# A cross-interaction network on one core: W1 and W2 loaded with h on the partitions, in rows of 256 bytes, instead of being turned on TensorE

## The chip, the core and the metric

The kernel runs on one core of one Trainium2 chip. The metric is the device time of one execution in microseconds (us); three runs of the kernel before gave a median of 1092.18 us (1091.85 to 1092.72). One more execution was profiled; its trace is what the rows below come from.

## The reference, cut to what matters

```python
# input: (B=512, F=64, D=16);  W0: (128, 64*64), W1, W2: (128, 128*64);  b*: (128,)
x_vec = input
for W, b in ((W0, b0), (W1, b1), (W2, b2)):
    z = einsum('bhd,bfd->bhfd', x_vec, input).reshape(B, h * f, D)
    x_vec = einsum('oc,bcd->bod', W, z) + b[None, :, None]
    outs.append(x_vec.sum(axis=2))
y = concatenate(outs, axis=1)            # (512, 3 * 128)
```

In layers 1 and 2 the sum over c is a sum over h (128 outputs of the layer before) and f (64 fields). TensorE sums over the partitions, so a weight that it uses must stand with h on the partitions; in memory a row o of W1 or W2 holds h times f values, f innermost.

## The kernel before, in words

A tile is 8 samples of the batch times 16 elements, 128 columns; four tiles are a group, and there are 16 groups (0 "first", 1 to 14 "inner", 15 "last"). On every engine the code is a hand-written order: `body(n, kind)` runs over the 64 steps e = 0 to 63 of a group, with tile j and chunk c from `divmod(e, 16)`; tables of steps such as `LATER_AT` say at which e other work stands. Engines meet through semaphores.

Layer 0 makes products z of two fields (SyncE copies rows of xg into z, GpSimd multiplies, L453), which TensorE multiplies with W0 into the bank l0 (`layer0`, 17 tiles of z to a group, every second one split by ScalarE, L526, and VectorE, L718, into an upper and a lower part). The result is split into x1h and x1l.

Layer 1: W1 lies in SBUF as w1h and w1l (upper and lower part), 16 chunks of 4 fields times 128 outputs. A chunk of a tile is three matmuls of 512 columns (`chunk`, `by_parts`, L913) into one of four banks y; then each of its four fields is scaled with x0t and added up, for five chunks of 16 by ScalarE (`multiply`, L673) and GpSimd (L461 to L474), for the others by VectorE (`add_fields`, L769; for chunks 3 and 15 ScalarE scales in place, L662, and VectorE adds, L754).

Layer 2 needs only the sum over the elements. For each tile `layer2` (L1033) makes x2 times the inputs, which ScalarE puts into gram (L563). After each quarter of the batch `quarter` (L1021) multiplies gram with w2t, 64 matmuls of 128 columns in fp32, each of two passes in the trace, with `w2t[:, f, :]` stationary: eight parts of eight fields between the chunks of steps 18 to 25 of groups 4, 8 and 12, and the last quarter at the very end. ScalarE's L571 then reads the sum.

The start: SyncE loads W1 in eight parts of 512 KB, in rows of 4 KB, into w1raw, which is the space of w2t, with o on the partitions (L387). Each chunk is turned by four transposes on TensorE (`turn_w1`, L968) into l2p, from which ScalarE makes w1h (`w1_upper`, L588) and VectorE w1l (`w1_lower`, L777). Two chunks are turned ahead (`W1_AHEAD`); each of steps 0 to 13 of group 0 turns one more ahead of its chunk, and chunk c of tile 0 waits for w1l of c. ScalarE loads W2 into w2raw, the space of gram, at steps 0, 1, 3, 4, 6, 7, 9 and 10 of group 0 (`load_w2`, L595). At steps 14 to 29 of group 0 TensorE turns W2 (`turn_w2`, L1010) and ScalarE copies it into w2t (`w2_out`, L582). Tile 0 of group 0 is done with the group's first 128 columns, whose layer 0 was made early; the other 384 (LATER) have their layer 0 at steps 3 to 13 of tile 0, with SyncE's copies held until the first six parts of W1 have landed, and tile 1 waits for their x1h and x1l (L735, step 14 on VectorE).

Of the kernel before, what the change touches and what calls it, by code (L numbers as in the profile page):

```python
# [12 lines left out]
B, F, D = 512, 64, 16  # L13
# [64 lines left out]
W2_AT = 14  # L78
# [6 lines left out]
W2_LOAD_AT = [k * 3 // 2 for k in range(W_PARTS)]  # L85
# [23 lines left out]
def layer2_at(n, j):  # L109

    return LAYER2_AT + 2 if n == 0 and j == 1 else LAYER2_AT


# [5 lines left out]
def cin_kernel(nc, x, w0, b0, w1, b1, w2, b2, out):  # L119
    with ExitStack() as ctx:  # L120
# [12 lines left out]
        w2t = sb("w2t", [P, F, O])  # L133
# [32 lines left out]
        w1raw = w2t[:].rearrange("p f o -> p (f o)")  # L166
        w2raw = gram[:].rearrange("p f b -> p (f b)")
# [4 lines left out]
        w0raw = w2raw[:, 0:F * F]  # L172
# [3 lines left out]
        w0pair, w0pair_left = w2raw[:, F * O - (ZT - 1) * P:], scratch[:, 4 * F:4 * F + ZCOPIES * ZLAST]  # L176
# [25 lines left out]
        w1_turned = sem("w1_turned")  # L202
# [10 lines left out]
        w2_turned = sem("w2_turned")  # L213
        w2_kept = sem("w2_kept")
# [144 lines left out]
        def _(sp):  # L359
# [68 lines left out]
        def _(pool):  # L428
# [13 lines left out]
            nc.gpsimd.memset(w2raw[:, F * F:(F + F // 2) * F], 0.0).then_inc(w0_spare_set, 1)  # L442
# [61 lines left out]
        def _(act):  # L504
# [74 lines left out]
            def w2_out(c):  # L579

                act.wait_ge(w2_turned, c + 1)
                nc.scalar.copy(w2t[:, CF * c:CF * c + CF, :], l2p[:, c % 2, :].rearrange("p (f o) -> p f o", o=O)) \  # L582
                    .then_inc(w2_kept, 1)
# [12 lines left out]

            def body(n, kind):
                act.wait_ge(x0t_made, 2 * n + 1)
                for e in range(TILES * CHUNKS):
# [4 lines left out]
                    if kind == "first" and e in W2_LOAD_AT:  # L604
                        load_w2(W2_LOAD_AT.index(e))
# [101 lines left out]
        def _(dve):  # L707
# [146 lines left out]
            for r in range(W0_STEPS - 1):  # L854
                if r == W0_STEPS - 2:
# [9 lines left out]
                          at(w2raw, F * F - F * s0, [-F, n], [F + 1, half - 1]))  # L865
# [38 lines left out]
        def _(pe):  # L904
# [53 lines left out]
            def turn_w1(k):  # L958

                if k == 0:  # L960
                    pe.wait_ge(w1_loaded, 16 * W1_FIRST)
                    pe.wait_ge(w1_rest_loaded, 16 * (W_PARTS - W1_FIRST))
                    pe.wait_ge(early_left_lowered, 1)
                    pe.wait_ge(early_z_made, W0_STEPS - 1)
                if k >= 2:
                    pe.wait_ge(w1l_made, k - 1)
                for i in range(CF):
                    last = nc.tensor.transpose(l2p[:, k % 2, i * O:(i + 1) * O],  # L968
                                               w1raw.rearrange("o (h f) -> o f h", f=F)[:, CF * k + i, :], ident[:])
                last.then_inc(w1_turned, 1)  # L970

# [32 lines left out]
            def turn_w2(c):  # L1004
                if c >= 2:
                    pe.wait_ge(w2_kept, c - 1)
                else:
                    pe.wait_ge(w1l_made, CHUNKS)
                for k in range(CF):
                    last = nc.tensor.transpose(l2p[:, c % 2, k * O:(k + 1) * O],  # L1010
                                               w2raw.rearrange("o (h f) -> o f h", f=F)[:, CF * c + k, :], ident[:])
                last.then_inc(w2_turned, 1)
# [55 lines left out]
            for k in range(W1_AHEAD):  # L1068
                turn_w1(k)
            pe.wait_ge(wh_made, W0_STEPS)  # L1070

            def body(n, kind):
                for e in range(TILES * CHUNKS):
# [9 lines left out]
                    if kind == "first" and e + W1_AHEAD < CHUNKS:  # L1083
                        turn_w1(e + W1_AHEAD)
# [5 lines left out]
                    if kind == "first" and W2_AT <= e < W2_AT + CHUNKS:  # L1090
                        if e == W2_AT:
                            pe.wait_ge(w2_loaded, 16 * W_PARTS)
                        turn_w2(e - W2_AT)
                    if c == layer2_at(n, j) and (kind != "first" or j > 0):
                        if kind == "first" and j == 1:
                            pe.wait_ge(w2_kept, CHUNKS)
                        layer2(tile - 1, (j - 1) % 2)
# [49 lines left out]
```

## Time and profile before

| what | value |
|---|---|
| median of three runs | 1092.18 us (1091.85 to 1092.72) |
| the profiled execution | 1091.6 us |
| span of its trace | 1089.5 us |
| TensorE busy (matmul) | 1064.6 us, 98% of the span |
| VectorE, GpSimd, ScalarE busy | 877.3, 859.6, 710.3 us |
| mean share of the DMA engines in group 0's first tile (26 to 60 us) | 0.87 |

About 2 us of the profiled execution lie outside the span. PE stands for TensorE's matmuls and PEld for its loads of stationary operands, which overlap with them; DVE is VectorE, ACT ScalarE, POOL GpSimd, SP SyncE, and a q behind an engine's name its issuing of DMAs. Times in a trace count from the span's start. Before some 120 us the engines wait for each other and for transfers; after that TensorE has hardly a gap until the last quarter.

### The profile page before, as it was taken

The page shows a single profiled execution, that of the slowest core. Times are in us where ns is not written, and L with a number is a line of the kernel's source. Part 1 is how long each engine was busy: PE and PEld are TensorE (multiplying, and loading weights), DVE is VectorE, ACT ScalarE, POOL GpSimd, SP SyncE. Part 2 cuts the span into 40 slices and gives each one's busy share as a digit, 9 for nine tenths or more (in the row PEclk, how much of TensorE's full clock was granted, in tenths as well). Part 3 has the DMA queues.
Part 4 walks back from the last instruction along what each step waited for, and adds up shares of the span by engine and source line. Part 5 has one row for each costly group of instructions (what it writes and reads, how often), then busy time and mean ns, then how long its engine had stood idle before and what let it go on. Part 6 is the DMA issues. An engine that isn't in the chain of part 4 may idle for free.

```text
span 1089.5 us, 18056 instructions
## 1 busy us (share of the span) xinstructions
PE 1064.6 (98%) x4783; PEld 803.5 (74%) x4783; DVE 877.3 (81%) x2673; ACT 710.3 (65%) x2447; POOL 859.6 (79%) x727
## 2 busy tenths in 40 slices
PE   5999999999999999999999999999999999999997
PEld 5777777777778777777778777777778877777676
DVE  5768989889874888989894798989886598888881
ACT  4666767676764767767673676777675576767770
POOL 2668997989884897989985799898987589898550
PEclk9999999999999999999999999999999999999998
DMA  7942423332322323323241232433332133320000
GB/s 275 245 92 81 101 71 71 96 76 78 66 70 58 76 78 69 85 57 97 66 87 40 56 97 66 88 84 69 94 79 59 47 69 97 76 79 28 1 23 8
DMA packets 108327, 85.88 MB, mean 79 GB/s; under 512 B 71040, under 2 KB 73824, under 8 KB 108096
## 3 DMA queue, kind: packets, MB, share of 16 engines
q1 hardware_dynamic: 106832, 78.17, 29.3%
q10 hardware_dynamic: 1392, 6.55, 1.9%
q8 instruction: 38, 0.62, 0.2%
q14 instruction: 65, 0.53, 0.2%
HBM read 14.75 MB, written 0.79 MB: 14 GB/s over the span
## 4 chain that ended last, share of the span: by engine, by line
PE 90%; DVE 3%; ACT 2%; DMA 2%; POOL 1%; issue 1%; ACTq 0%; SPq 0%; DVEq 0%; POOLq 0%
PE y L913 62%; PE l L934 9%; PE l L913 8%; PE xt L1021 5%; PE l2p L1033 4%; DVE acc L769 2%; DMA gram<-in_L_rec_W_dram 1%; PE l2p L1010 1%; ACT y L662 1%; DMA z<-xg 1%; ACT prod L673 1%; POOL z L453 1%; DVE gram L851 1%; PE l L922 0%; POOL pacc L463 0%
## 5 line engine op out<-in xcount | busy, mean ns | idle before, releaser
L769 DVE SCALAR_TENSOR_TENSOR acc<-y,x0t,acc 128x128 f32<-128x128 f32 x2048 | 559.8, 341 | 101.8 <-PE y L913 99.1
L673 ACT ACTIVATE prod<-y,x0t 128x128 f32<-128x128 f32 x1280 | 365.8, 379 | 157.4 <-PE y L913 148.6
L913 PE MATMUL y<-w1h,x1h 128*128 128x512 f32 x1024 | 464.6, 454 | 2.2 <-DVE acc L769 1.4
L913 PE MATMUL y<-w1h,x1l 128*128 128x512 f32 x1024 | 402.1, 393 | 0.0
L913 PE MATMUL y<-w1l,x1h 128*128 128x512 f32 x1024 | 400.6, 391 | 0.0
L453 POOL TENSOR_TENSOR z<-z,xg 128x512 f32<-128x512 f32 (+2 forms) x272 | 352.5, 1300 | 32.8 <-DMA z<-xg 32.8
L463 POOL TENSOR_TENSOR pacc<-pacc,prod 128x512 f32<-128x512 f32 x192 | 268.0, 1396 | 79.7 <-ACT prod L673 78.3
L913 PEld LDWEIGHTS y<-w1h,x1h 128*128 128x128 f32 x1024 | 193.2, 189 | 96.8 <-issue 26.5
L662 ACT ACTIVATE y<-y,x0t 128x128 f32<-128x128 f32 x512 | 142.6, 342 | 157.4 <-PE y L913 157.2
L913 PEld LDWEIGHTS y<-w1l,x1h 128*128 128x128 f32 x1024 | 192.8, 188 | 59.3 <-issue 28.8
L913 PEld LDWEIGHTS y<-w1h,x1l 128*128 128x128 f32 x1024 | 192.1, 188 | 43.0
L754 DVE TENSOR_TENSOR acc<-y,acc 128x512 f32<-128x512 f32 x128 | 88.3, 690 | 64.6 <-ACT y L662 61.4
L718 DVE TENSOR_TENSOR zl<-z,zh 128x512 fp32r<-128x512 f32 (+1 forms) x128 | 126.9, 991 | 7.1 <-ACT zh L526 4.5
L934 PE MATMUL l<-z,w0t 128*128 128x512 f32 (+1 forms) x256 | 128.8, 584 | 0.0
L469 POOL TENSOR_TENSOR pacc<-pacc,acc 128x512 f32<-128x512 f32 x63 | 87.4, 1387 | 42.4 <-DVE acc L754 34.5
L461 POOL TENSOR_TENSOR pacc<-prod 128x512 f32<-128x512 f32 x64 | 90.0, 1406 | 37.7 <-ACT prod L673 37.5
L526 ACT CAST zh<-z 128x512 fp32r<-128x512 f32 (+1 forms) x128 | 81.4, 636 | 10.9 <-POOL z L453 7.7
L652 ACT ACTIVATE bd<-x0t,own_half 128x64 f32<-128x64 f32 x256 | 69.1, 359 | 0.0
L1021 PEld LDWEIGHTS xt<-gram,w2t 128*128 128x128 f32 x512 | 62.3, 195 | 3.6 <-ACT sums L565 1.5
L1021 PE MATMUL xt<-gram,w2t 128*128 128x128 f32 x512 | 62.7, 279 | 0.8 <-ACT sums L565 0.8
L767 DVE TENSOR_SCALAR acc<-y,x0t 128x128 f32<-128x128 f32 x192 | 54.9, 341 | 0.0
L934 PEld LDWEIGHTS l<-z,w0t 128*128 128x128 f32 x256 | 47.8, 188 | 9.6
(85 smaller groups left out, 673.0 us busy)
## 6 DMA issues: line engine op xcount, KB each, us to landing
z<-xg SPq DMA_DIRECT2D x480, 128.0 KB, 2.4
w2t<-in_L_rec_W_dram SPq DMA_DIRECT2D x8, 512.0 KB, 7.1
gram<-in_L_rec_W_dram ACTq DMA_DIRECT2D x8, 512.0 KB, 7.4
xg<-in_r_input_dram SPq DMA_DIRECT2D x30, 128.0 KB, 3.8
z<-xg SPq DMA_DIRECT2D x32, 96.0 KB, 5.9
z<-xg SPq DMA_DIRECT2D x15, 192.0 KB
gram<-in_L_rec_W_dram ACTq DMA_DIRECT2D x1, 2048.0 KB, 9.2
out_dram<-z SPq DMA_DIRECT2D x4, 192.0 KB, 1.9
```

The lines of the kernel that those rows point to most:

```text
L453: nc.gpsimd.tensor_tensor(to[0:rows, :], to[0:rows, :], xg[0:rows, cols], ALU.mult).then_inc(z_made, 1)
L461: nc.gpsimd.tensor_tensor(pacc[:], prod[:, 0], prod[:, 1], ALU.add).then_inc(pool_step, 1)
L463: nc.gpsimd.tensor_tensor(pacc[:], pacc[:], prod[:, h % HSLOTS], ALU.add).then_inc(pool_step, 1)
L469: nc.gpsimd.tensor_tensor(pacc[:], pacc[:], acc[:, slot], ALU.add).then_inc(pool_step, 1)
L662: last = nc.scalar.activation(of, of, ACT.Copy, scale=x0t[:, j, f:f + 1])
L673: last = nc.scalar.activation(prod[:, h % HSLOTS, k, :], y[c % YB][:, k * O:(k + 1) * O], ACT.Copy, scale=x0t[:, j, f:f + 1])
L718: nc.vector.tensor_tensor(zl[:, i % ZLSLOTS, cols], zin(n, t), zh[:, zhslot(n, t), cols].bitcast(F32), ALU.subtract).then_inc(zl_made, 1)
L754: nc.vector.tensor_tensor(to, y[c % YB][:], to, ALU.add).then_inc(acc_step, 1)
L769: ins = nc.vector.scalar_tensor_tensor(out=to, in0=of, scalar=x0t[:, j, f:f + 1], in1=b1r[:] if m == 0 else to, op0=ALU.mult, op1=ALU.add)
L913: ins = nc.tensor.matmul(to, stationary, moving, start=(first and k == 0), stop=(last and k == 2))
L934: nc.tensor.matmul(l0[:, cols], w0t[:, WHOLE.index(t), :], zin(n, t), start=(t == 0), stop=False).then_inc(z_used, 1)
L1021: last = nc.tensor.matmul(l2, w2t[:, f, :], gram[:, f, :], start=(f == 0), stop=(f == F - 1))
```

## The change

W1 and W2 are loaded by their DMAs straight into the layout with h on the partitions: `w2t` is now [h, o, f], part k of a load is 16 outputs o, and each piece that the DMA moves is one (o, h) row of 64 fields, 256 bytes (before, 4 KB). So the transposes `turn_w1` and `turn_w2` are gone, and `w2_out` with them. `w1_upper` and `w1_lower` take their chunk from SBUF, from w2t with a step of 64 elements from one o to the next, and write the same w1h and w1l. ScalarE's first one waits for all eight parts of W1. W2 goes into w2t itself, after W1 has been used up, in group 1 (steps 4, 11, ..., 53), and `quarter` reads `w2t[:, :, f]`, a step of 64 elements from column to column. `quarter(1)` waits for the load.

```diff
-W2_AT = 14
-W2_LOAD_AT = [k * 3 // 2 for k in range(W_PARTS)]
+W2_LOAD_AT = [4 + 7 * k for k in range(W_PARTS)]
-        w2t = sb("w2t", [P, F, O])
+        w2t = sb("w2t", [P, O, F])
-        w1raw = w2t[:].rearrange("p f o -> p (f o)")
+        w1raw = w2t[:].rearrange("p o f -> p f o")
...
-                    part = slice(k * F * O // W_PARTS, (k + 1) * F * O // W_PARTS)
-                    sp.dma_start(w1raw[:, part], w1[:, part]).then_inc(w1_loaded if k < W1_FIRST else w1_rest_loaded, 16)
+                    part = slice(k * O // W_PARTS, (k + 1) * O // W_PARTS)
+                    sp.dma_start(w2t[:, part, :], w1[part, :].rearrange("o (h f) -> h o f", f=F)) \
+                        .then_inc(w1_loaded if k < W1_FIRST else w1_rest_loaded, 16)
...
             def w1_upper(k):
-                act.wait_ge(w1_turned, k + 1)
-                nc.scalar.copy(w1h[:, k, :], l2p[:, k % 2, :]).then_inc(w1h_made, 1)
+                if k == 0:
+                    act.wait_ge(w1_loaded, 16 * W1_FIRST)
+                    act.wait_ge(w1_rest_loaded, 16 * (W_PARTS - W1_FIRST))
+                nc.scalar.copy(w1h[:, k, :].rearrange("p (f o) -> p f o", o=O),
+                               w1raw[:, CF * k:CF * k + CF, :]).then_inc(w1h_made, 1)
             def load_w2(k):
                 if k == 0:
-                    act.wait_ge(w0l_made, W0_STEPS - 1)
-                act.dma_start(w2raw[:, part], w2[:, part]).then_inc(w2_loaded, 16)
+                    act.wait_ge(w1l_made, CHUNKS)
+                act.dma_start(w2t[:, part, :], w2[part, :].rearrange("o (h f) -> h o f", f=F)).then_inc(w2_loaded, 16)
...
-                    if kind == "first" and e in W2_LOAD_AT:
+                    if n == 1 and e in W2_LOAD_AT:
                         load_w2(W2_LOAD_AT.index(e))
...
             def w1_lower(k):
-                nc.vector.tensor_tensor(w1l[:, k, :], l2p[:, k % 2, :], w1h[:, k, :].bitcast(F32),
-                                        ALU.subtract).then_inc(w1l_made, 1)
+                split = w1h[:, k, :].bitcast(F32).rearrange("p (f o) -> p f o", o=O)
+                nc.vector.tensor_tensor(w1l[:, k, :].rearrange("p (f o) -> p f o", o=O),
+                                        w1raw[:, CF * k:CF * k + CF, :], split, ALU.subtract).then_inc(w1l_made, 1)
...
             def quarter(q, part, fields_kept):
                 if part == 0:
+                    if q == 1:
+                        pe.wait_ge(w2_loaded, 16 * W_PARTS)
...
-                    last = nc.tensor.matmul(l2, w2t[:, f, :], gram[:, f, :], start=(f == 0), stop=(f == F - 1))
+                    last = nc.tensor.matmul(l2, w2t[:, :, f], gram[:, f, :], start=(f == 0), stop=(f == F - 1))
```

(`turn_w1`, `turn_w2`, `w2_out`, `layer2_at` and the semaphores between them are taken out; w2raw, which also holds W0, is named w0stage.)

On TensorE, where group 0 begins, there stood (L968 turns W1, L913 is a chunk):

```order
L985 MATMUL l0<-zh,w0left 128x128
L968 MATMUL l2p<-ident,w2t 128x128 x12
L913 MATMUL y0<-w1h,x1h 128x512
L913 MATMUL y0<-w1l,x1h 128x512
L913 MATMUL y0<-w1h,x1l 128x512
L968 MATMUL l2p<-ident,w2t 128x128 x4
L913 MATMUL y1<-w1h,x1h 128x512
```

and now stands (L901 is the chunk):

```order
L959 MATMUL l0<-zh,w0left 128x128
L901 MATMUL y0<-w1h,x1h 128x512
L901 MATMUL y0<-w1l,x1h 128x512
L901 MATMUL y0<-w1h,x1l 128x512
L901 MATMUL y1<-w1h,x1h 128x512
```

The twelve transposes ahead of the first chunk and the four ahead of each later one are gone; nothing takes their place on TensorE.

On VectorE, at the same place, there stood (L777 makes w1l, L769 and L767 add up chunk 1, L718 splits z):

```order
L735 SCALAR_TENSOR_TENSOR x1l<-l0,b0c,x1h 128x128
L777 TENSOR_TENSOR w1l<-l2p,w1h 128x512 x4
L769 SCALAR_TENSOR_TENSOR acc<-y1,x0t,b1r 128x128
L767 TENSOR_SCALAR acc<-y1,x0t 128x128 x3
L718 TENSOR_TENSOR zl<-z,zh 128x384
```

and now stands:

```order
L722 SCALAR_TENSOR_TENSOR x1l<-l0,b0c,x1h 128x128
L765 TENSOR_TENSOR w1l<-w2t,w1h 128x512 x4
L756 SCALAR_TENSOR_TENSOR acc<-y1,x0t,b1r 128x128
L754 TENSOR_SCALAR acc<-y1,x0t 128x128 x3
L705 TENSOR_TENSOR zl<-z,zh 128x384
```

The order is as before; the first operand of the sixteen instructions that make w1l is w2t in SBUF where it was l2p in PSUM.

On ScalarE, in group 1, the first of the eight loads of W2 now stands between work of step 3 and step 4 (L649 and L660 scale chunks); the rows that load W2 in group 0 are gone:

```order
L550 ACTIVATE x1h<-l0,b0c 128x128
L649 ACTIVATE y3<-y3,x0t 128x128 x4
L584 DMA w2t<-in_L0_rec_W2_dram 128x16x64
L660 ACTIVATE prod<-y0,x0t 128x128 x4
```

So the eight loads of W2 have moved from group 0 to group 1, into the order of the steps 4, 11, ..., 53.

## Rows read from the trace of the kernel before

**Rows 1.** The page: engines' busy time, and the chain that ended last

```profile
PE 1064.6 (98%) x4783; PEld 803.5 (74%) x4783; DVE 877.3 (81%) x2673; ACT 710.3 (65%) x2447; POOL 859.6 (79%) x727
PE 90%; DVE 3%; ACT 2%; DMA 2%; POOL 1%; issue 1%; ACTq 0%; SPq 0%; DVEq 0%; POOLq 0%
```

**Rows 2.** Windows: length, busy us (instructions), granted clock, DMA share, GB/s

```profile
26.00:60.00 34.00, 31.17 (x153) 24.98 (x153) 25.44 (x63) 20.91 (x57) 20.99 (x19) 1.00 0.87 214
60.00:119.00 59.00, 57.69 (x257) 43.33 (x257) 43.05 (x121) 40.77 (x125) 47.23 (x39) 1.00 0.39 93
```

**Rows 3.** Timeline of PE (start, us, instruction): transposes, and starts of tiles 0, 1 and 4

```profile
23.26 1.42 PE L968 MATMUL l2p<-ident,w2t 128*128 128x128 f32 x8 [0.89 <-issue]
26.17 0.48 PE L913 MATMUL y<-w1h,x1h 128*128 128x512 f32 x1
...
59.78 0.47 PE L913 MATMUL y<-w1h,x1h 128*128 128x512 f32 x1 [0.46 <-issue]
...
119.21 0.39 PE L913 MATMUL y<-w1h,x1h 128*128 128x512 f32 x1
```

**Rows 4.** The chain that ended last, in order of time: start, us, what

```profile
24.75 0.70 DVE w1l L777
...
33.58 7.98 DMA z<-xg
...
63.99 0.55 PE l2p L1010 x4
...
88.41 0.68 PE l L913 x3
...
90.44 0.86 PE l L934 x2
...
100.62 0.64 PE l2p L1033 x4
```

**Rows 5.** Groups by shape on DVE, 0 to 120 us: count, busy us, mean ns, idle before

```profile
L777 DVE TENSOR_TENSOR w1l<-l2p,w1h 128x512 fp32r<-128x512 f32 x16 | 10.9, 683 | 3.8 <-ACT w1h L588 3.8
L718 DVE TENSOR_TENSOR zl<-z,zh 128x512 fp32r<-128x512 f32 x8 | 9.9, 1238 | 0.6 <-ACT zh L526 0.5
L851 DVE TENSOR_TENSOR gram<-gram 128x256 f32<-128x256 f32 x8 | 5.0, 629 | 0.3
L888 DVE TENSOR_TENSOR w0l<-gram,w0h 128x256 fp32r<-128x256 f32 x4 | 1.5, 422 | 0.1
```

**Rows 6.** Timeline of PEld: eight loads from contiguous columns, eight with 256 bytes between

```profile
15.84 0.97 PEld L977 LDWEIGHTS l<-prod,gram 128*128 128x128 f32 x8
...
23.23 1.25 PEld L968 LDWEIGHTS l2p<-ident,w2t 128*128 128x128 f32 x8 [1.00 <-issue]
```

**Rows 7.** Groups on PE and PEld, 0 to 120 us, columns as in rows 5

```profile
L968 PE MATMUL l2p<-ident,w2t 128*128 128x128 f32 x64 | 11.8, 310 | 1.8 <-DVE w1l L777 0.9 <-issue 0.9
L968 PEld LDWEIGHTS l2p<-ident,w2t 128*128 128x128 f32 x64 | 11.1, 245 | 3.7 <-issue 2.1 <-DVE w1l L777 0.4
L977 PEld LDWEIGHTS l<-prod,gram 128*128 128x128 f32 x24 | 2.9, 191 | 0.0
```

**Rows 8.** The chain: one part of a quarter and the chunk behind it

```profile
319.52 1.78 PE xt L1021 x16
321.31 0.70 PE y L913 x3
```

**Rows 9.** The page's DMA issues: KB each, median us to landing

```profile
z<-xg SPq DMA_DIRECT2D x480, 128.0 KB, 2.4
w2t<-in_L_rec_W_dram SPq DMA_DIRECT2D x8, 512.0 KB, 7.1
xg<-in_r_input_dram SPq DMA_DIRECT2D x30, 128.0 KB, 3.8
```

**Rows 10.** Line 402, SyncE's loads of xg: issue time ns min/median/max

```profile
L402 SPq DMA_DIRECT2D xg<-in_r_input_dram x30: 650/912/1532, 53.0 to 938.7; - x30
```

**Rows 11.** Groups on ACT, as in rows 5

```profile
L588 ACT CAST w1h<-l2p 128x512 fp32r<-128x512 f32 x16 | 9.4, 592 | 3.5 <-PE l2p L968 3.4
```

More of the change, by code:

```diff
@@ L106, in zslot @@
     return t % ZSLOTS
-def layer2_at(n, j):
-    return LAYER2_AT + 2 if n == 0 and j == 1 else LAYER2_AT
 def last_in(t, slots):
@@ L163, in cin_kernel @@
         sums2_from_1 = sums[:].rearrange("p l b -> p (l b)")[:, 2 * B - QB:]
-        w1raw = w2t[:].rearrange("p f o -> p (f o)")
-        w2raw = gram[:].rearrange("p f b -> p (f b)")
+        w1raw = w2t[:].rearrange("p o f -> p f o")
+        w0stage = gram[:].rearrange("p f b -> p (f b)")
         zfirst = [prod[:, i] for i in range(HSLOTS)] + [acc[:, 0]]
@@ L171, in cin_kernel @@
         xraw = zflat[0:GROUP_B, 0:2 * F * D]
-        w0raw = w2raw[:, 0:F * F]
+        w0raw = w0stage[:, 0:F * F]
         zturned = zflat[:, ZSLOTS * GROUP - (ZT - 1) * P:]
@@ L175, in cin_kernel @@
         xturned, zturned_left = scratch[:, 0:2 * F], scratch[:, 2 * F:2 * F + ZCOPIES * ZLAST]
-        w0pair, w0pair_left = w2raw[:, F * O - (ZT - 1) * P:], scratch[:, 4 * F:4 * F + ZCOPIES * ZLAST]
+        w0pair, w0pair_left = w0stage[:, F * O - (ZT - 1) * P:], scratch[:, 4 * F:4 * F + ZCOPIES * ZLAST]
         outs = zflat[:, 0:(B // P) * L * O].rearrange(
@@ L201, in cin_kernel @@
         pair_step = sem("pair_step")
-        w1_turned = sem("w1_turned")
         w1_rest_loaded = sem("w1_rest_loaded")
@@ L212, in cin_kernel @@
         w0left_made = sem("w0left_made")
-        w2_turned = sem("w2_turned")
-        w2_kept = sem("w2_kept")
         xg_loaded = sem("xg_loaded")
@@ L441, in _ @@
                                     pattern=[[D, TILE_B]], channel_multiplier=-1).then_inc(consts_made, 1)
-            nc.gpsimd.memset(w2raw[:, F * F:(F + F // 2) * F], 0.0).then_inc(w0_spare_set, 1)
+            nc.gpsimd.memset(w0stage[:, F * F:(F + F // 2) * F], 0.0).then_inc(w0_spare_set, 1)
             def product(n, t):
@@ L577, in row_out @@
                 nc.scalar.copy(outs[:, r, :], l0[:, 0:L * O]).then_inc(outs_made, 1)
[L579 to L583, printed above, removed]
             def w1_upper(k):
-                act.wait_ge(w1_turned, k + 1)
-                nc.scalar.copy(w1h[:, k, :], l2p[:, k % 2, :]).then_inc(w1h_made, 1)
+                if k == 0:
[3 more added lines that the diff above has]
+                               w1raw[:, CF * k:CF * k + CF, :]).then_inc(w1h_made, 1)
             def load_w2(k):
                 if k == 0:
-                    act.wait_ge(w0l_made, W0_STEPS - 1)
-                part = slice(k * F * O // W_PARTS, (k + 1) * F * O // W_PARTS)
-                act.dma_start(w2raw[:, part], w2[:, part]).then_inc(w2_loaded, 16)
+                    act.wait_ge(w1l_made, CHUNKS)
+                part = slice(k * O // W_PARTS, (k + 1) * O // W_PARTS)
+                act.dma_start(w2t[:, part, :], w2[part, :].rearrange("o (h f) -> h o f", f=F)).then_inc(w2_loaded, 16)
             def body(n, kind):
@@ L617, in body @@
                         scale(tile, j, c)
-                    if kind == "first" and W2_AT <= e - 1 < W2_AT + CHUNKS:
-                        w2_out(e - 1 - W2_AT)
-                    if c == layer2_at(n, j) + 1 and (kind != "first" or j > 0):
+                    if c == LAYER2_AT + 1 and (kind != "first" or j > 0):
                         before = (n * TILES + (j - 1) + QG * TILES) % (QG * TILES) if kind != "first" else j - 1
@@ L864, in _ @@
                           at(w0raw, F - s0, [-1, n], [F + 1, half - 1]),
-                          at(w2raw, F * F - F * s0, [-F, n], [F + 1, half - 1]))
+                          at(w0stage, F * F - F * s0, [-F, n], [F + 1, half - 1]))
                 add_pairs(at(w0pair, F * s0, [F, n], [1, half]),
@@ L956, in turn_w0 @@
                 last.then_inc(prep_made, 1)
[L958 to L970, printed above, removed]
             def early_layer0(r):
@@ L1002, in turn_row @@
                 last.then_inc(turned, 1)
[L1004 to L1012, printed above, removed]
             def quarter(q, part, fields_kept):
@@ L1067, in _ @@
             early_left()
-            for k in range(W1_AHEAD):
-                turn_w1(k)
             pe.wait_ge(wh_made, W0_STEPS)
@@ L1082, in body @@
                         pe.wait_ge(l2_used, (n // QG if kind == "inner" else 0) + 1)
-                    if kind == "first" and e + W1_AHEAD < CHUNKS:
-                        turn_w1(e + W1_AHEAD)
                     if kind == "first" and j == 0:
@@ L1089, in body @@
                         turn_row(ROWS_AT.index(e))
[L1090 to L1096, printed above, removed]
+                    if c == LAYER2_AT and (kind != "first" or j > 0):
                         layer2(tile - 1, (j - 1) % 2)
```

## The prediction

> **What bounds the kernel now.** I read the page first: TensorE is busy for 98% of the span, and the chain that ended last is TensorE for 90% [rows 1]. From that alone, taking transposes off TensorE saves their time. But an average hides stages, so I read windows and starts of tiles next. Tile 0 of group 0 runs from 26.17 to 59.78, 33.6 us, tiles 1 to 3 from 59.78 to 119.21, 59.4 us [rows 3], while a tile without z work beside it holds 16 chunks of about 0.70 us, some 11 us [rows 8]. In 26 to 60 TensorE shows 31.2 us busy, yet VectorE has 25.4 and the DMA engines 0.87 [rows 2], and the chain goes there through a transfer of z (7.98 us at 33.58), not through TensorE alone [rows 4]. So I count three stages apart: tile 0, where several engines are near their limit; tiles 1 to 3, where TensorE is; and the other fifteen groups, where TensorE alone counts and each nanosecond added to it is added to the end. I then looked for rows that show what a step of 256 bytes costs a reader of SBUF, since the change brings three such readers.
>
> **W1's arrival.** Before, TensorE starts to turn W1 at 23.26 [rows 3], so W1 has landed by then. The same 4 MB now come as 16,384 pieces of 256 bytes instead of 1,024 of 4 KB. The nearest rows: 128 KB in 64 pieces of 2 KB (z from xg) land after 2.4 us, 128 KB in 2,048 pieces of 64 bytes (xg) after 3.8 [rows 9], so 2,000 more pieces take 1.4 us more. Each of the eight parts has 2,048 pieces. Lower bound: the pieces hide behind the bytes, nothing. Upper bound: 8 x 1.4 = 11 us. I take 4 us, nearer to the lower end since bytes and pieces are moved by the same engines together: W1 is there at 27. The issues, 0.65 to 1.5 us for as many pieces [rows 10], total at most 12 us from 8.6 on and are done before.
>
> The Trainium skill, page "DMA: Bandwidth & Descriptors", section "Specifications", asks for at least 512 bytes in a transfer for the full rate and says that smaller ones are read, modified and written. By that W1 would come at some half of its rate, near the upper bound; no row here has pieces of 256 bytes.
>
> **Tile 0.** TensorE loses 16 blocks of four transposes, 0.55 us each [rows 4], and ScalarE and VectorE no longer wait for them. But w1l changes its price. Before, it reads one operand from PSUM and takes 683 ns [rows 5]. Now both are in SBUF, one with 256 bytes between its elements. A subtraction with both in SBUF, contiguous, of 256 elements takes 422 ns (L888); an addition of 256 with steps of 260 bytes takes 629 (L851) [rows 5]. The step costs 207 ns per 256 elements, so 414 per 512: 683 + 414 = 1.10 us. Bounds: 0.68, if one strided operand is free, and 2 x 629 = 1.26. Besides, an operation with both operands in SBUF and GpSimd at work beside it averages 1,238 ns for 512 elements (L718) [rows 5], 0.55 above 683; GpSimd is busy for 21 of 34 us here [rows 2], so I add half, 0.25. That makes 1.35 us, with 0.68 and 1.8 as ends. ScalarE's copies, 592 ns from PSUM [rows 11], have no row for a strided read from SBUF: between 0.6 and, with VectorE's increase, 1.0 us; ScalarE has 13 us to spare in this stage [rows 2], so only the first is on the path.
>
> VectorE's work: of 25.44 us in 26 to 60, fourteen w1l are 9.6, so 15.9 are other work [rows 2, 5]. Sixteen at 1.35 are 21.6; the sum is 37.5 us. It starts at 27 + 1.0 = 28.0 instead of 24.75 [rows 4]; with 2 us of waits (z copies begin later, but no longer share the DMA engines with W2) tile 1 starts at 67.5 instead of 59.78: **7.7 us later**. TensorE's freed 9 us buy nothing here; VectorE is late next.
>
> **Tiles 1 to 3.** Fourteen blocks of four transposes go, and the waits for ScalarE's copies between them. What is left for TensorE: 48 chunks at 0.70, 33.6; eight tiles of z at 0.86 and eight at 0.68 for group 1, 12.3; three `layer2` at 0.64 and what follows them, about 0.85 each, 2.5; turning fields and the last tile of z 0.6 [rows 4, 8]: 49.0. GpSimd needs 47.2 of its own [rows 2], so it nearly binds; I take 50.5 instead of 59.4: **8.9 us saved**. Group 1 then starts at 118.0 instead of 119.2.
>
> **W2 in group 1.** Eight issues on ScalarE, 0.65 to 1.5 us each going by the loads of xg [rows 10], in front of ScalarE's multiplies, for which the banks y wait. Hidden while ScalarE (65% busy [rows 1]) is ahead; TensorE has four banks, 2.8 us, to run on. Bounds 0 and 8 x 0.65 = 5; I take **1 us**. `quarter(1)` is three groups later, so its wait costs nothing.
>
> **The quarters.** Each of 512 passes of L1021 loads 128 columns of w2t, now with 256 bytes from column to column. A part of sixteen takes 1.78 us on the chain, 0.111 each [rows 8], and that is also the pitch of loads from contiguous columns, (0.97 - 0.19) / 7 [rows 6, 7]: the loads, not the matmuls, set it. L968 loads W1 with the very step that w2t has now, 64 elements: (1.25 - 0.25) / 7 = 0.143 [rows 6, 7], and the eight matmuls on them take (1.42 - 0.31) / 7 = 0.159 with the first gap in it [rows 3, 7], 0.31 being the mean length of one. I take 0.146. So 512 x 0.0345 = **17.7 us more**, in stages where TensorE has no idle time to absorb it; VectorE and GpSimd only idle longer. Bounds: 0, if the load hides behind a matmul of two passes; by the blocks of 0.55 for four (0.138) 13.6; if each load's extra length (245 against 191 ns, rows 7) shows in full, 27.6.
>
> The Trainium skill, page "TensorE: Matmul & The Clock Gate", section "LDWEIGHTS (loading the stationary operand)", gives a load's time from its number of columns alone; by that the step would be free and this term nothing. Rows 7 disagree, 245 against 191 ns for as many columns.
>
> **The sum.** +7.7 - 8.9 + 1 + 17.7 = +17.5 us on a span of 1089.5 and a profiled execution of 1091.6; the median of the runs is 0.6 above that. 1092.2 + 17.5 = 1109.7; I say 1109.
>
> **Rivals.**
> 1. *VectorE and GpSimd take the stride for nothing* (w1l at 0.95 us, with the contention alone). For it: no row has one strided operand beside a contiguous one; in L851 both are strided and in the same tile. Tile 0 then needs 15.2 + 15.9 = 31 us on VectorE and tile 1 starts near 61: 1102 to 1103.
> 2. *Pieces of 256 bytes are paid one by one.* W1 is there at 34, 7 us later, and z's copies, held until six parts are there, as well: 1116, up to 1120 if VectorE also waits for GpSimd in full (1.8 us). For it: 64-byte pieces cost 1.4 us a part; against it: those rows include no queue of parts.
> 3. *The strided loads hide in the quarters*, the other side: the pitch stays 0.111, the 17.7 us fall away, and the time is 1092, no change; with rival 1 as well, 1085, faster. It decides from the point where a pass's matmul takes longer than 0.146. For it: in L968's blocks the matmul is one pass of another kind; against it: the pitch of L1021 equals that of bare contiguous loads. The skill's rule on columns would have this result.
> 4. That the change does not do what it says is no rival: both transposes are gone from TensorE's order, and what reads w2t is there with its step. Only the gain in tile 0 is in doubt, above.
>
> **How the numbers follow.** The forecast 0.53 (its own range 1103 to 1114), rival 1 0.18, rival 2 0.17, rival 3 0.12, of which 0.05 faster, 0.04 within 0.2% and 0.03 slower (a part of the 17.7 left). From the forecast's bounds and rivals 1 and 2, the range is 1098 to 1121; it leaves out rival 3 and the end of rival 2. About 0.2% is what a measurement of this kernel can tell from no change; that is 2.2 us. Faster 0.05, within it 0.05, slower 0.90.
>
> **What would show it.** In the changed kernel's profile: the parts of a quarter near 2.3 us on the chain, the last quarter longer by some 4 us; w1l near 1.1 us where GpSimd is idle and more beside it; tile 1 starting near 67, with VectorE busy throughout tile 0; group 1 starting near 118; W1 landed near 27. Wrong would be: quarters unchanged in pitch, then rival 3; w1l under 0.8, then rival 1; the first chunk after 35, then rival 2; TensorE idle in group 1 at the issues of W2 by more than 5 us.

## The result, and the profile after

| | before | after |
|---|---|---|
| median of four runs, side by side | 1092.45 us (1091.85 to 1093.49) | 1148.47 us (1148.06 to 1148.94) |
| span of the profiled execution | 1089.5 us | 1146.0 us |

The changed kernel is 5.1% slower: the ratio is 1.0512, 95% interval 1.0494 to 1.0530. The sign was right; the size was not: 1109 was forecast with a range to 1121, and the loss is 56 us instead of 17.

I read the trace of the changed kernel in the order of the prediction, by stages. In the new lines, a chunk is L901, `w1_upper` L576, `w1_lower` L765, a quarter L987, the load of W1 L378. First the timeline of TensorE (start, us, instruction): the first matmul of tile 0, of tile 1, of group 1 and of group 2; it answers to [rows 3].

```profile
34.07 0.76 PE L901 MATMUL y<-w1h,x1h 128*128 128x512 f32 x1 [9.42 <-DVE w1l L765]
...
74.75 0.47 PE L901 MATMUL y<-w1h,x1h 128*128 128x512 f32 x1 [0.59 <-issue]
...
124.39 0.39 PE L901 MATMUL y<-w1h,x1h 128*128 128x512 f32 x1
...
186.47 0.39 PE L901 MATMUL y<-w1h,x1h 128*128 128x512 f32 x1
```

Against [rows 3], tile 0 starts 7.9 us later and takes 40.7 us instead of 33.6; tiles 1 to 3 take 49.6 instead of 59.4; group 1 takes 62.1 where its counterpart, from 119.21 to 181.04, took 61.8. So at group 2 the changed kernel is 5.4 us behind, of 56. The rest lies in the four quarters. The chain that ended last (start, us, what) shows it, beside [rows 8]:

```profile
324.95 3.40 PE xt L987 x16
328.35 0.70 PE y L901 x3
329.05 3.40 PE xt L987 x16
```

A part of sixteen passes takes 3.40 us instead of 1.78, 0.2125 us a pass instead of 0.111, and a chunk beside it is unchanged. Each of the groups 4, 8 and 12 is 12.9 us longer (87.8 against 74.8), and the last quarter, which has nothing beside it, 12.2. The groups on the two pages (count, busy us, mean ns, idle before) say the same of the loads, first in the changed kernel, then in the kernel before:

```profile
L987 PEld LDWEIGHTS xt<-gram,w2t 128*128 128x128 f32 x512 | 114.6, 311 | 2.5 <-ACT sums L557 1.5
```

```profile
L1021 PEld LDWEIGHTS xt<-gram,w2t 128*128 128x128 f32 x512 | 62.3, 195 | 3.6 <-ACT sums L565 1.5
```

The start, on the chain, and then in windows (length; busy us and instructions of PE, PEld, DVE, ACT and POOL; granted clock, DMA share, GB/s), as in [rows 2]:

```profile
21.02 2.52 SPq L378
...
23.58 7.73 DMA w2t<-in_L_rec_W_dram
...
31.38 1.07 ACT w1h L576
...
32.47 1.35 DVE w1l L765
```

```profile
20.00:24.00 4.00, 3.23 (x29) 3.02 (x28) 2.94 (x10) 2.55 (x9) 0.00 (x0) 1.00 1.35 219
26.00:34.00 8.00, 0.00 (x0) 0.00 (x0) 1.53 (x2) 2.62 (x3) 2.01 (x2) 0.55 1.02 198
34.00:75.00 41.00, 33.75 (x90) 20.52 (x91) 40.20 (x63) 26.39 (x56) 28.35 (x21) 0.75 0.35 79
75.00:124.00 49.00, 48.93 (x200) 34.86 (x200) 40.88 (x120) 32.65 (x111) 46.96 (x38) 1.00 0.43 104
```

The last piece of W1 lands at 31.3, its eighth issue having begun only at 23.6: each issue holds SyncE for some 2.3 us. While W1 comes in pieces of 256 bytes the DMA engines are busy without a pause and move 219 GB/s (20 to 24 us). In the kernel before, with rows of 4 KB, they moved 419:

```profile
16.00:20.00 4.00, 3.57 (x32) 3.38 (x32) 3.76 (x10) 2.63 (x10) 0.00 (x0) 1.00 1.03 419
```

At 219 GB/s a part of 512 KB takes 2.4 us, about as long as an issue is held, so issues and transfers go at one pace. An issue of as many pieces took 0.37 us in group 1, where the loads stood some 7 us apart, so it is not slow in itself; that it waits for the transfers ahead of it is the likelier reading, and is not shown.

While TensorE waits, its granted clock falls to 0.55, a mix of its two levels (1.2 and 2.4 GHz), and it is 0.75 in tile 0. But in tile 0 VectorE is busy for 40.20 of 41 us: it sets the end there. In tiles 1 to 3 TensorE is busy throughout, as forecast.

The groups of VectorE and ScalarE up to 120 us, beside [rows 5, 11], and after them the lower part of z of the same shape in the kernel before:

```profile
L765 DVE TENSOR_TENSOR w1l<-w2t,w1h 128x512 fp32r<-128x512 f32 x16 | 23.8, 1500 | 7.7 <-ACT w1h L576 7.7
L705 DVE TENSOR_TENSOR zl<-z,zh 128x384 fp32r<-128x384 f32 x8 | 8.1, 1008 | 0.0
L576 ACT CAST w1h<-w2t 128x512 fp32r<-128x512 f32 x16 | 17.3, 1100 | 6.3 <-DMA w2t<-in_L_rec_W_dram 6.3
```

```profile
L718 DVE TENSOR_TENSOR zl<-z,zh 128x384 fp32r<-128x384 f32 x8 | 5.6, 696 | 6.2 <-ACT zh L526 3.9 <-PE l L934 2.3
```

### The profile page after: what moved, and what is told of

The parts are those of the page before. It is cut to its first block, busy times and chain, and to the rows that moved or that the text cites. A ratio compares the mean times of both kernels' runs of the same rounds, so it can differ in the third digit from the quotient of the medians.

```text
span 1146.0 us, 17779 instructions
## 1 busy us (share of the span) xinstructions
PE 1109.0 (97%) x4655; PEld 842.2 (73%) x4655; DVE 890.5 (78%) x2673; ACT 708.9 (62%) x2431; POOL 867.1 (76%) x727
## 4 chain that ended last, share of the span: by engine, by line
PE 86%; DVE 4%; issue 3%; POOL 2%; SPq 1%; ACT 1%; DMA 1%; ACTq 0%; DVEq 0%; POOLq 0%
PE y L901 57%; PE xt L987 10%; PE l L922 8%; PE l L901 7%; PE l2p L999 3%; DVE acc L756 2%; SPq L378 1%; DVE w1l L765 1%; POOL z L445 1%; POOL pacc L455 1%; DMA w2t<-in_L_rec_W_dram 1%; ACT y L649 1%; POOL pacc L453 1%; DVE zl L705 1%; DVE acc L741 0%
## 5 line engine op out<-in xcount | busy, mean ns | idle before, releaser
L901 PE MATMUL y<-w1h,x1h 128*128 128x512 f32 x1024 | 466.9, 456 | 14.5 <-DVE w1l L765 11.6
L660 ACT ACTIVATE prod<-y,x0t 128x128 f32<-128x128 f32 x1280 | 365.7, 380 | 182.8 <-PE y L901 172.8
L901 PE MATMUL y<-w1h,x1l 128*128 128x512 f32 x1024 | 403.8, 394 | 0.0
L901 PE MATMUL y<-w1l,x1h 128*128 128x512 f32 x1024 | 403.0, 394 | 0.0
L445 POOL TENSOR_TENSOR z<-z,xg 128x512 f32<-128x512 f32 (+2 forms) x272 | 359.4, 1326 | 33.3 <-DMA z<-xg 33.3
L901 PEld LDWEIGHTS y<-w1h,x1h 128*128 128x128 f32 x1024 | 193.5, 189 | 117.3 <-issue 38.0
L649 ACT ACTIVATE y<-y,x0t 128x128 f32<-128x128 f32 x512 | 142.6, 342 | 158.5 <-PE y L901 158.5
L901 PEld LDWEIGHTS y<-w1l,x1h 128*128 128x128 f32 x1024 | 194.0, 189 | 59.7 <-issue 28.8
L901 PEld LDWEIGHTS y<-w1h,x1l 128*128 128x128 f32 x1024 | 193.4, 189 | 43.2
L461 POOL TENSOR_TENSOR pacc<-pacc,acc 128x512 f32<-128x512 f32 x63 | 87.8, 1393 | 40.5 <-DVE acc L741 32.6
L987 PEld LDWEIGHTS xt<-gram,w2t 128*128 128x128 f32 x512 | 114.6, 311 | 2.5 <-ACT sums L557 1.5
L987 PE MATMUL xt<-gram,w2t 128*128 128x128 f32 x512 | 113.8, 379 | 0.7 <-ACT sums L557 0.7
```

The lines of the kernel that those rows point to most:

```text
L445: nc.gpsimd.tensor_tensor(to[0:rows, :], to[0:rows, :], xg[0:rows, cols], ALU.mult).then_inc(z_made, 1)
L461: nc.gpsimd.tensor_tensor(pacc[:], pacc[:], acc[:, slot], ALU.add).then_inc(pool_step, 1)
L649: last = nc.scalar.activation(of, of, ACT.Copy, scale=x0t[:, j, f:f + 1])
L660: last = nc.scalar.activation(prod[:, h % HSLOTS, k, :], y[c % YB][:, k * O:(k + 1) * O], ACT.Copy, scale=x0t[:, j, f:f + 1])
L901: ins = nc.tensor.matmul(to, stationary, moving, start=(first and k == 0), stop=(last and k == 2))
L987: last = nc.tensor.matmul(l2, w2t[:, :, f], gram[:, f, :], start=(f == 0), stop=(f == F - 1))
```

## Experiments

### One part alone: only the quarters' layout

The kernel before, with both transposes left in place; only w2t has o ahead of f, so that a quarter reads every 64th element.

```diff
-        w2t = sb("w2t", [P, F, O])
+        w2t = sb("w2t", [P, O, F])
...
-                    last = nc.tensor.matmul(l2, w2t[:, f, :], gram[:, f, :], start=(f == 0), stop=(f == F - 1))
+                    last = nc.tensor.matmul(l2, w2t[:, :, f], gram[:, f, :], start=(f == 0), stop=(f == F - 1))
```

> The kernel before, with one part of the change alone: w2t lies as [h, o, f] (ScalarE's copies of the turned W2 write with a step of 256 bytes) and the quarters read their stationary operand with that step; W1 and W2 are loaded and turned as before. Theory A, the step alone doubles the pitch of the quarters' 512 passes: 1092.4 + 512 x (0.2125 - 0.111) = 1144 us, with the parts of sixteen at 3.40 us on the chain. Rival B, the pitch comes from how the change fills w2t or from its transfers running beside it: the parts stay between 1.8 and 2.4 us and the time between 1092 and 1111.

Measured: 1146.28 us, ratio 1.0493 (1.0477 to 1.0508). Its chain in the first quarter:

```profile
323.65 3.40 PE xt L1022 x16
```

The layout alone gives 53.7 of the 56 us, at the same 3.40 us a part. By the spans it is 54.9 us, and 50.8 of them lie behind the start of group 2, which comes 4.1 us later than in the kernel before (185.14 against 181.04). Of these 4.1, 2.8 are tile 1, which went from 26.7 to 29.5 us, as ScalarE's copies into that layout went from 0.6 to 1.1 us and stand on its chain. Another 2.3 are a later first chunk (28.51 against 26.17 us) although nothing was changed ahead of it, so single traces of the start differ by some 2 us; tile 0 is 1.0 shorter.

### The other part alone: the quarters read a row again

The changed kernel, where a quarter's stationary operand is 128 elements in a row.

```diff
-                    last = nc.tensor.matmul(l2, w2t[:, :, f], gram[:, f, :], start=(f == 0), stop=(f == F - 1))
+                    last = nc.tensor.matmul(l2, w2t[:].rearrange("p o f -> p (o f)")[:, f * O:(f + 1) * O], gram[:, f, :], start=(f == 0), stop=(f == F - 1))
```

> The changed kernel with the quarters' stationary operand read from 128 contiguous columns of w2t; these are other values than layer 2 needs, so the layer's sums are not the reference's, the work is the same. Theory A, the step of the quarters is 51 of the 56 us: 1148.5 - 51 = 1097 us, 4 to 6 above the kernel before, and the parts of sixteen at 1.78 us. Rival B, as above: parts above 2.4 us and a time near 1148.

Measured: 1098.21 us, ratio 1.0053 (1.0038 to 1.0067); a part takes 1.78 us again.

```profile
325.10 1.78 PE xt L987 x16
```

So all the rest of the change costs 5 to 6 us, and 50 us hang on the step at which the quarters read w2t. Tile 0 still takes 40.5 us here (34.22 to 74.70); the next runs start from this kernel.

### How the price depends on the step

The changed kernel, with three of the quarters read at another step in each of their eight parts: 1, 2, 4, 8, 16, 32, 63 and 64 elements. The first quarter has the strided operand stationary, the second transposes it, the third has it moving.

```diff
+STEPS = (1, 2, 4, 8, 16, 32, 63, 64)
...
+                    step = STEPS[part]
+                    of = flat[:, f % step:f % step + step * (O - 1) + 1:step]
+                    if q == 1:
+                        last = nc.tensor.matmul(l2, of, gram[:, f, :], start=(f == 0), stop=(f == F - 1))
+                    elif q == 2:
+                        for _ in range(2):
+                            last = nc.tensor.transpose(l2, of, ident[:])
+                    else:
+                        last = nc.tensor.matmul(l2, gram[:, f, :], of, start=(f == 0), stop=(f == F - 1))
```

> The changed kernel, with its eight parts of a quarter reading w2t at steps of 1, 2, 4, 8, 16, 32, 63 and 64 elements in turn: in the first quarter as the stationary operand of the fp32 matmul, in the second as that of a transpose (two to a field, so sixteen to a part as well), in the third as the moving operand of the fp32 matmul, with gram stationary. The sums of these quarters are not the reference's. Theory A (a load is slowed by each new 16-byte line of SBUF, as the Trainium skill, page SBUF - State Buffer, section Specifications, has it): first quarter 1.8 us a part at steps 1 and 2 and 3.4 from step 4 on, 63 like 64. Rival B (banks: a step that is a power of two is what hurts): 63 near 1.8, and a growth over 8, 16, 32, 64. Second quarter: 2.35 us (0.147 each) at step 64 if a transpose loads faster than a pass of an fp32 matmul, as before; 3.4 if it was its surroundings that made it so. Third quarter: 1.8 us at each step if the moving operand has time to spare in a two-pass matmul; 3.4 at the long steps if it reads through the same limit.

The parts on the chain, for steps 1, 2, 4 and 64 with the operand stationary (L995), 32 and 64 as a transpose (L998), 1, 2 and 4 as the moving operand (L1000):

```profile
325.31 1.78 PE xt L995 x16
...
327.79 1.88 PE xt L995 x16
...
330.36 3.61 PE xt L995 x16
...
353.07 3.40 PE xt L995 x16
...
605.77 1.79 PE xt L998 x16
...
611.61 2.32 PE xt L998 x16
...
849.70 1.78 PE xt L1000 x16
...
852.18 1.82 PE xt L1000 x16
...
854.70 3.63 PE xt L1000 x16
```

For the fp32 matmul the price is a jump, not a slope. Up to a step of 2 elements (8 bytes) it is nothing or 0.1 us a part, from 4 elements (16 bytes) on the part takes 3.4 to 3.7 us at every step, and it makes no difference which of the two operands is strided. Sixteen transposes at the same steps take 1.75 to 1.96 us, and 2.32 only at 64. So a transpose is no proxy for a pass of an fp32 matmul: my row for the price was of the wrong kind of instruction.

The Trainium skill, page "SBUF — State Buffer", section "Specifications (TRN2)", has lines of 16 bytes and wants two hits in each for the full bandwidth; the jump between 8 and 16 bytes agrees with that. By its words alone the transposes should pay too, and from 4 to 32 elements they do not.

### Which read sets the pitch

The same three quarters, now with 128, 112, 96, 80, 64, 48, 32 and 16 moving columns: first W2 stationary at every 64th element (L996), then stationary in a row (L992), then gram stationary and W2 moving at every 64th element (L994).

```diff
+COLUMNS = (128, 112, 96, 80, 64, 48, 32, 16)
...
+                    if q == 2:
+                        last = nc.tensor.matmul(l2[:, 0:n], flat[:, f * O:(f + 1) * O], gram[:, f, 0:n], **ends)
+                    elif q == 3:
+                        last = nc.tensor.matmul(l2[:, 0:n], gram[:, f, :], w2t[:, 0:n, f], **ends)
+                    else:
+                        last = nc.tensor.matmul(l2[:, 0:n], w2t[:, :, f], gram[:, f, 0:n], **ends)
```

> The changed kernel with three forms of the quarter, part by part with 128, 112, 96, 80, 64, 48, 32 and 16 moving columns: the first quarter with W2 as the stationary operand at every 64th element, the second with W2 as the stationary operand in a row, the third with gram as the stationary operand and W2 moving at every 64th element; the last quarter is unchanged. The columns left out are not computed. If the read of the strided operand sets the pitch (twice 128 columns at 0.83 ns, 212 ns), the first quarter's parts of 16 stay at 3.4 us whatever the count of moving columns, and the third's fall with the count from 3.5 us to that of the stationary read, about 1.8 us, at 64. If the matmul itself is slower whatever is read, the first quarter's parts fall with the columns too. The second quarter's parts stay near 1.8 us if its stationary read sets the pitch, and fall below if the moving columns do.

From the chain, the parts with 128 and 16 columns of the first form, 16 of the second, and 128, 112, 80 and 64 of the third:

```profile
325.20 3.40 PE xt L996 x16
...
357.24 3.26 PE xt L996 x16
...
617.33 1.69 PE xt L992 x16
...
854.78 3.51 PE xt L994 x16
...
858.99 3.08 PE xt L994 x16
...
866.98 2.23 PE xt L994 x16
...
869.91 1.77 PE xt L994 x16
```

With the strided operand stationary the pitch does not follow the moving columns: the load sets it, 212 ns for 128 columns, 1.66 ns each, against 111 ns or 0.87 each in a row. With it moving, 16 columns fewer take 0.43 us off a part, 27 ns off a pass, 1.7 ns a column, until the contiguous load is the longer at 64 columns. Both readers pay about double for each column at this step. No order of the operands avoids it; another place in memory does.

### W1's small pieces

The kernel with contiguous quarter reads, and W1 loaded in rows of 4 KB as before.

```diff
-                    part = slice(k * O // W_PARTS, (k + 1) * O // W_PARTS)
-                    sp.dma_start(w2t[:, part, :], w1[part, :].rearrange("o (h f) -> h o f", f=F)) \
+                    part = slice(k * F * O // W_PARTS, (k + 1) * F * O // W_PARTS)
+                    sp.dma_start(w2t[:].rearrange("p o f -> p (o f)")[:, part], w1[:, part]) \
```

> As the kernel with contiguous quarters, and W1 loaded in rows of 4 KB as before the change, into the same space (so w1h and w1l hold values of W1 in wrong places); everything that reads w2t keeps its step. Theory A, the 256-byte rows delay W1 from 23 to 31 us and tile 0 with it: the first chunk starts 7 to 8 us earlier, near 26.5, tile 1 near 67 instead of 74.8, and the time is 1097 - 6 to 8 = 1090. Rival B, tile 0 is bound by VectorE and GpSimd whenever W1 comes: tile 1 starts less than 3 us earlier, and the time is 1095 or more.

Measured: 1090.94 us, ratio to the kernel before 0.9982 (0.9972 to 0.9992), 7.3 less than with the small pieces. On TensorE's timeline the first chunk starts 6.9 us earlier than at 34.22. The eight issues of the load (issue ns min/median/max, first and last start us), here and then in the changed kernel:

```profile
27.33 0.67 PE L901 MATMUL y<-w1h,x1h 128*128 128x512 f32 x1 [2.73 <-DVE w1l L765]
```

```profile
L378 SPq DMA_DIRECT2D w2t<-in_L_rec_W_dram x8: 328/572/1509, 8.1 to 13.7; - x8
```

```profile
L378 SPq DMA_DIRECT2D w2t<-in_L_rec_W_dram x8: 379/2324/3812, 8.1 to 23.6; - x8
```

The pieces of 256 bytes are nearly all of the late start, 6.9 of 7.9 us, and they show as issues that hold the queue. Tile 0 takes 39.5 us here (27.33 to 66.82) although the granted clock is 0.91 in it, not 0.75: the lower clock accounts for at most 1 of its 7 us.

### What makes tile 0 long: the step

The kernel with contiguous quarter reads, small pieces again; ScalarE and VectorE read 512 elements of w2t in a row.

```diff
-                               w1raw[:, CF * k:CF * k + CF, :]).then_inc(w1h_made, 1)
+                               w2t[:].rearrange("p o f -> p (o f)")[:, k * CHUNK:(k + 1) * CHUNK].rearrange("p (f o) -> p f o", o=O)).then_inc(w1h_made, 1)
...
-                                        w1raw[:, CF * k:CF * k + CF, :], split, ALU.subtract).then_inc(w1l_made, 1)
+                                        w2t[:].rearrange("p o f -> p (o f)")[:, k * CHUNK:(k + 1) * CHUNK].rearrange("p (f o) -> p f o", o=O), split, ALU.subtract).then_inc(w1l_made, 1)
```

> The kernel of the run with contiguous quarter reads (1098.2 us, tile 0 from 34.1 to 74.6), and in it ScalarE's and VectorE's 16 reads each of W1 are of 512 elements in a row instead of every 64th; so w1h and w1l hold other values of W1 than they should, and the numbers computed are not the reference's. If the stride is what made tile 0 longer (40.5 us against 33.6 before), ScalarE's copy falls from 1.10 to about 0.6 us and VectorE's difference from a mean of 1.5 to 0.7 to 0.9 us, tile 0 takes 33 to 35 us and the time is about 1092. If tile 0 is long because the layer 0 operations around it and GpSimd set its pace, the instructions get shorter, tile 0 stays at 38 us or more and the time at 1096 or more.

Measured: 1093.23 us, ratio 1.0009 (0.9999 to 1.0018); tile 0 takes 36.7 us (32.96 to 69.66). Neither expectation held in full. ScalarE's copy takes 0.62 us, but the differences fell less than expected; one line of them (ns min/median/max, first and last start):

```profile
L765 DVE TENSOR_TENSOR w1l<-w2t,w1h x16: 677/1482/1760, 32.0 to 66.3; 128x512 fp32r<-128x512 f32 x16
```

Two prices stand in that row, so I set VectorE's timeline in the changed kernel (start, us) beside GpSimd's:

```profile
44.25 1.06 DVE L765 TENSOR_TENSOR w1l<-w2t,w1h 128x512 fp32r<-128x512 f32 x1
...
45.82 1.82 DVE L765 TENSOR_TENSOR w1l<-w2t,w1h 128x512 fp32r<-128x512 f32 x1
```

```profile
45.55 1.28 POOL L453 TENSOR_TENSOR pacc<-prod 128x512 f32<-128x512 f32 x1 [3.56 <-ACT prod L660]
46.80 1.67 POOL L445 TENSOR_TENSOR z<-z,xg 128x384 f32<-128x384 f32 x1
```

With GpSimd idle the strided difference takes 1.06 us; with GpSimd at work through it, 1.82. In the contiguous run the two are 0.68 and mostly 1.49 (of the twelve with GpSimd beside them one takes 1.05, and two, which began just ahead of a GpSimd instruction or in its last 0.1 us, take 0.69). So the step costs 0.4 us and GpSimd mostly 0.8, and ten of the sixteen differences in the changed kernel take over 1.3 us.

### What makes tile 0 long: SBUF beside GpSimd

The last kernel, where the difference takes its first operand from PSUM, as before the change.

```diff
-                                        w2t[:].rearrange("p o f -> p (o f)")[:, k * CHUNK:(k + 1) * CHUNK].rearrange("p (f o) -> p f o", o=O), split, ALU.subtract).then_inc(w1l_made, 1)
+                                        l2p[:, k % 2, :].rearrange("p (f o) -> p f o", o=O), split, ALU.subtract).then_inc(w1l_made, 1)
```

> The kernel of the last run with contiguous reads of W1 (1093.2 us; tile 0 from 32.9 to 69.6, 36.7 us), and in it VectorE's 16 differences take their first operand from PSUM instead of from w2t in SBUF, so that the lower parts are not those of W1 and the numbers computed are not the reference's. There the difference took 0.69 us where no GpSimd instruction ran beside it and 1.49 us where one did, and in the kernel before, with the operand in PSUM, 0.67 to 0.69 us with and without. If SBUF beside GpSimd is what is left of tile 0's loss, all 16 take 0.7 us, tile 0 takes 32 to 34.5 us and the time is 1089 to 1091. If tile 0's pace is set by GpSimd's products and by layer 0, the differences get as short, but tile 0 stays above 36 us and the time at 1093.

Measured: 1087.40 us, ratio 0.9945 (0.9928 to 0.9962).

```profile
L765 DVE TENSOR_TENSOR w1l<-l2p,w1h x16: 675/678/692, 32.0 to 60.1; 128x512 fp32r<-128x512 f32 x16
```

All sixteen take 0.68 us, whatever GpSimd does, and tile 0 takes 30.5 us (32.99 to 63.47), less than the 32 to 34.5 expected, and the time lies below the 1089 to 1091 expected. So of the changed kernel's 40.7 us, SBUF beside GpSimd takes 6.2 (36.7 less 30.5), the step 3.8 (40.5 less 36.7), and 0.2 are left. What the change takes out of tile 0, the turns on TensorE and the loads of W2, gives back 3.1 against 33.6 before; no run parts the two. On the chain before stood a transfer of z of 7.98 us [rows 4], while W2 was loading. In the kernel of the next section, which still turns W1 on TensorE, that transfer takes 4.65 us and tile 0 is 30.85, nearly as short as here. So the 3.1 us are not shown to be TensorE's.

The Trainium skill, page "SBUF — State Buffer", section "SBUF: two separate sides", says that a VectorE operation with two SBUF inputs and a GpSimd operation that reads SBUF exclude each other, and that the later one waits in full. That such a pair costs time, and one operand in PSUM does not, the trace shows (1.49 against 0.68 us). The contiguous run also shows the wait. Two GpSimd instructions and the difference that began in each (start, us):

```profile
45.59 1.33 POOL L445 TENSOR_TENSOR z<-z,xg 128x384 f32<-128x384 f32 x1
49.27 1.59 POOL L455 TENSOR_TENSOR pacc<-pacc,prod 128x512 f32<-128x512 f32 x1
```

```profile
45.97 1.50 DVE L765 TENSOR_TENSOR w1l<-w2t,w1h 128x512 fp32r<-128x512 f32 x1
49.64 1.76 DVE L765 TENSOR_TENSOR w1l<-w2t,w1h 128x512 fp32r<-128x512 f32 x1
```

GpSimd had 0.95 and 1.21 us left when they began, and both end 0.55 us after it did. All ten differences longer than 0.69 us end 0.55 us after the GpSimd instruction in which they began, with 0.50 to 1.21 us of it left. So the price is not a fixed 0.8 us: it is what was left of the other instruction, less some 0.13. That agrees with a full wait, as far as the spans of GpSimd, which are rough in a trace, can tell.

### A version that beats both

The kernel before, W1 as it was; only W2 is not turned on TensorE. It lands in rows of 256 bytes in the columns 64 to 127 of gram, which no tile writes before group 2, half of the outputs in group 0 and half in group 1, and ScalarE copies it into the old layout of w2t. `turn_w2` and its waits are taken out. So the step is paid sixteen times on ScalarE, which has idle time, not 512 times on TensorE, which has none.

```diff
-                act.dma_start(w2raw[:, part], w2[:, part]).then_inc(w2_loaded, 16)
+                act.dma_start(gram[:, 16 * k:16 * k + 16, F:QB],
+                              w2[F * half + 16 * k:F * half + 16 * k + 16, :].rearrange("o (h f) -> h o f", f=F)) \
+                    .then_inc(w2_loaded, 16)
...
-                nc.scalar.copy(w2t[:, CF * c:CF * c + CF, :], l2p[:, c % 2, :].rearrange("p (f o) -> p f o", o=O)) \
-                    .then_inc(w2_kept, 1)
+                nc.scalar.copy(w2t[:, 8 * c:8 * c + 8, F * half:F * half + F],
+                               gram[:, :, F + 8 * c:F + 8 * c + 8].rearrange("p o f -> p f o")).then_inc(w2_kept, 1)
```

> The kernel before with W1 as it was (rows of 4 KB, turned by TensorE) and only W2 not turned by TensorE: it lands in 256-byte rows in the columns 64 to 127 of gram, which no tile writes before group 2, half of W2's outputs in group 0 and half in group 1, and ScalarE copies it in 16 copies of 512 elements into the old layout of w2t (f ahead of o), so that the quarters read a row of 128 outputs as before. If the layout that the quarters read is the whole cost of leaving the turn out and the tiles 1 to 3 give back what they gave in the changed kernel (59.4 to 49.6 us), the time is about 1092.4 - 9.8 = 1082.6, between 1081 and 1085, and the quarter parts stay at 1.78 us. If ScalarE's 16 copies of 1.1 us are in the way of its products (it is busy 42 of 61 us in a group), tiles 1 to 3 and group 1 give half or more of it back and the time is 1087 to 1093.

Measured: 1083.51 us (1083.29 to 1084.67), ratio 0.9921 (0.9907 to 0.9936): 0.8% faster than the kernel before, within the 1081 to 1085 expected. TensorE's first matmuls of tile 0, tile 1 and group 1; on the chain, the transfer of z in tile 0 and a quarter's part; and ScalarE's copies:

```profile
27.25 0.48 PE L911 MATMUL y<-w1h,x1h 128*128 128x512 f32 x1
...
58.10 0.47 PE L911 MATMUL y<-w1h,x1h 128*128 128x512 f32 x1 [1.69 <-issue]
...
109.08 0.39 PE L911 MATMUL y<-w1h,x1h 128*128 128x512 f32 x1
```

```profile
35.13 4.65 DMA z<-xg
...
318.83 1.78 PE xt L1011 x16
```

```profile
L577 ACT COPY w2t<-gram 128x512 f32<-128x512 f32 x16 | 18.3, 1146 | 0.0
```

Tiles 1 to 3 take 51.0 us, 8.4 less than before, and the quarters are as they were. Tile 0 is also 2.8 shorter (30.85), which I had not counted; its transfer of z is 3.3 us shorter on the chain, with half as much of W2 loading beside it. Group 1 takes 62.9, 1.0 more, with eight of the copies. That the time came out as expected is partly luck: tiles 1 to 3 gave 8.4 us instead of 9.8, and tile 0 made up for that and for group 1.

## Why the prediction was wrong, point by point

- **The quarters** were the step that failed, in size: +17.7 us forecast, with 27.6 as the upper bound, and some 51 measured (three times 12.9 and 12.2). The mechanism was right: the loads set the pitch, and TensorE has no idle time to absorb it. The pitch was 0.2125 us, not 0.146, because I took it from L968's transposes [rows 6, 7]. The bound had the same fault: it was built from that one row, so it bounded how much of a transpose's price would show, not what an fp32 pass would pay. I had noted that L968's matmul is "one pass of another kind" and used it only in favour of a smaller cost.
- **Rival 3**, quarters unchanged in pitch, fell with it, and with it the rule that a load's time goes by its columns alone (the Trainium skill, page "TensorE: Matmul & The Clock Gate", section "LDWEIGHTS (loading the stationary operand)"): 212 against 111 ns for the same 128 columns.
- **W1's arrival**: 27 forecast, 31.3 measured. My bounds, 0 and 11 us from before's 23, held it, but the value lay too near the lower end. I had said that the issues are done before the landing and took up to 1.5 us for each; they took 2.3 and stood on the path, at the pace of the transfers, 219 GB/s against 419. About half the rate, and so a value near the upper bound, stood beside my bounds, and I did not use it. Rival 2, pieces that cost time one by one, was nearer; its sign, a first chunk after 35, was missed by a microsecond.
- **Tile 0**: VectorE was late next, as said, and TensorE's freed time was not worth its 9 us. But w1l takes 1.50 us in the mean, not 1.35. The step's 1.06 us was forecast well (1.10), so rival 1, the stride for nothing, fell; the contention was 0.25 in my sum and 0.44 in the mean, because most of the differences begin while GpSimd is at work and end only after it. The lower parts of z with both operands in SBUF went from 696 to 1,008 ns as well, which I had not counted. ScalarE's copy takes 1.10 us, just above my upper end of 1.0, and does not matter beyond the first. Tile 1 starts 15.0 us later instead of 7.7, about half of it from W1's arrival.
- **Tiles 1 to 3** held: 49.6 us against 50.5 forecast, and a gain of 9.8 against 8.9.
- **W2's load in group 1** held: 0.25 us against 1, between its bounds; it is hidden.

By the forecast's own steps: 15.0 - 9.8 + 0.25 + 50.9 = 56.4 us, the difference of the spans being 56.5. Of the 39 us that the sum missed, 33 are the quarters and 7 the start.

## What to carry to other kernels

Before an operand's layout is changed to save a one-time turn, count how often it is read afterwards, on which engine, and take the price of a strided read from a row of the same kind of instruction in the same precision; if there is none, the upper bound is open, and one small run settles it. A stride is best paid once, by an engine with idle time, on the way to a layout that the bound engine reads in a row. And an operand that moves from PSUM to SBUF can cost more through the neighbour on GpSimd than through its step.

## What the hardware showed that I had not expected

- An fp32 matmul's price for a strided operand jumps between steps of 8 and 16 bytes, from 0.111 to 0.21 to 0.23 us a pass, for the stationary and the moving operand alike, and then stays there up to 256 bytes; transposes of the same operand stay at 0.11 to 0.12 us and reach 0.145 only at 256 bytes. Why the transposes are spared is open.
- A VectorE subtraction of 512 elements from SBUF took 0.68 us alone and mostly 1.49 beside GpSimd, ending 0.55 us after the GpSimd instruction in which it began; with one operand in PSUM it took 0.68 in both cases.
- With the DMA engines busy without a pause, W1 came at 219 GB/s in pieces of 256 bytes, and at up to 419 in rows of 4 KB. A load of 512 KB in 2,048 pieces of 256 bytes held its issuing queue for a median of 2.3 us when eight came one behind another, and 0.37 us in group 1, where they came some 7 us apart.
